# One written-out order of 248 letters in place of slots and places, in a pipelined cross-attention kernel

## What is computed

```python
# layer 0
x = attention(ln(x), ln(x), Wq1, Wkv1, Wo1, bo1) + x      # self-attention, 16 heads of 16, scale 1/8
x = attention(ln(x), ctx,   Wq2, Wkv2, Wo2, bo2) + x      # cross-attention, 16 heads of 16
h = ln(x) @ Wff1 + bff1;  lin, g = split(h)               # 256 -> 2 x 1024
x = (lin * (g * sigmoid(1.702 * g))) @ Wff2 + bff2 + x
# layer 1: one attention of x over the context, with its own projections
q, k, v = x @ Wq + bq, ctx @ Wk + bk, ctx @ Wv + bv       # one head, no scale
out = softmax(q @ k.T) @ v + x
```

## Time and profile before

| | us |
|---|---|
| median of 3 runs (1865.70 to 1873.52) | 1872.56 |
| the profiled execution, own time | 1862.73 |
| its span, first to last instruction | 1860.9 |
| busy in the span: PE | 1640.9 (88%) |
| DVE | 1111.0 (60%) |
| ACT | 978.3 (53%) |
| POOL | 265.7 (14%) |
| mean granted TensorE clock | 0.967 |

### The profile page before, as it was taken

How to read it: one execution, slowest core, us unless ns; L and a number is a source line. 1 busy time by engine, 2 the same in 40 slices (tenths; PEclk the granted TensorE clock), 3 DMA queues, 4 the chain that set the end, 5 groups by cost and what they waited for, 6 DMA issues and landing times.

```text
span 1860.9 us, 33823 instructions
## 1 busy us (share of the span) xinstructions
PE 1640.9 (88%) x12897; PEld 1037.2 (56%) x12897; DVE 1111.0 (60%) x2221; ACT 978.3 (53%) x2024; POOL 265.7 (14%) x344
## 2 busy tenths in 40 slices
PE   6799889898989989898998989899898989897877
PEld 5444444564646556564655656465555656464656
DVE  4556676747576575757656574756657575733332
ACT  3255656554656555565555545565554546554332
POOL 5210411201211020121102012100001010101110
PEclk9999999999999999999999999999999999998988
DMA  6904243335131412436121221335030220302200
GB/s 177 211 27 131 66 76 84 74 79 107 48 70 54 80 47 54 88 72 118 51 66 53 56 61 46 78 78 109 19 76 27 54 63 27 76 21 65 50 29 12
DMA packets 171647, 129.37 MB, mean 70 GB/s; under 512 B 40751, under 2 KB 161885, under 8 KB 171229
## 3 DMA queue, kind: packets, MB, share of 16 engines
q1 hardware_dynamic: 171421, 127.19, 29.2%
q10 hardware_dynamic: 64, 0.02, 0.0%
HBM read 78.92 MB, written 47.71 MB: 68 GB/s over the span
## 4 chain that ended last, share of the span: by engine, by line
PE 65%; DVE 21%; ACT 6%; issue 5%; DMA 2%; SPq 1%; ACTq 0%; POOL 0%; DVEq 0%; POOLq 0%
DVE mxh L1383 10%; PE ps_o L1732 10%; PE ps_last L1649 10%; PE ps_max L1705 9%; PE ps_s L1720 6%; PE ps_last L1658 6%; PE ps_pre L1513 4%; PE ps_cross L1617 3%; PE ps_pre L1521 3%; DVE mx L1307 3%; PE ps_cross L1603 2%; PE ps_last L1521 2%; ACT probs L1096 2%; PE ps_last L1687 2%; DVE hT L1342 1%
## 5 line engine op out<-in xcount | busy, mean ns | idle before, releaser
L1383 DVE TENSOR_REDUCE mxh<-ps_max 128x1 f32<-128x512 f32 x1024 | 667.8, 684 | 379.7 <-PE ps_max L1705 377.6
L1152 ACT ACTIVATE probs<-ps_s 128x512 f32<-128x512 f32 x1024 | 556.0, 598 | 316.3 <-PE ps_s L1720 310.7
L1705 PE MATMUL ps_max<-kst,qst 96*128 96x512 bf16 x1024 | 382.4, 390 | 86.1 <-DVE mxh L1383 71.0
L1720 PE MATMUL ps_s<-qst,kst 98*128 98x256 bf16 x2048 | 319.7, 278 | 1.2 <-ACT probs L1152 0.7
L1732 PE MATMUL ps_o<-probs,vg 128*17 128x256 f32 x4096 | 283.4, 393 | 6.4 <-ACT probs L1152 6.4
L1720 PEld LDWEIGHTS ps_s<-qst,kst 98*128 98x128 bf16 x2048 | 199.1, 99 | 92.2 <-issue 11.6
L1705 PEld LDWEIGHTS ps_max<-kst,qst 96*128 96x128 bf16 x1024 | 97.0, 97 | 229.2 <-DVE mxh L1383 170.2
L1096 ACT ACTIVATE probs<-ps_cross 77x512 f32<-77x512 f32 x224 | 133.5, 596 | 85.1 <-PE ps_cross L1603 85.1
L1732 PEld LDWEIGHTS ps_o<-probs,vg 128*17 128x17 f32 x4096 | 93.8, 98 | 136.6 <-issue 69.2
L1649 PE MATMUL ps_last<-y_hi,wff_hi 128*128 128x256 f32 x448 | 140.6, 314 | 24.5 <-DVE hT L1342 19.3
L1125 ACT ACTIVATE th<-ps_last,b_tanh 128x256 f32<-128x256 f32 x112 | 53.1, 474 | 160.4 <-PE ps_last L1649 160.4
(11 more groups left out here) (265 smaller groups left out, 2014.5 us busy)
## 6 DMA issues: line engine op xcount, KB each, us to landing
parts_s<-qk_parts SPq DMA_DIRECT2D x28, 384.0 KB, 3.1
o_s<-o_sb SPq DMA_DIRECT2D x64, 128.0 KB, 2.1
o_s<-o_sb SPq DMA_DIRECT2D x32, 256.0 KB, 2.2
oT<-o_s SPq DMA_DIRECT2D x62, 128.0 KB
den<-o_s SPq DMA_DIRECT2D x62, 128.0 KB
kst<-parts_s SPq DMA_DIRECT2D x16, 384.0 KB, 5.3
kst<-parts_s SPq DMA_DIRECT2D x48, 128.0 KB, 6.1
qst<-parts_s SPq DMA_DIRECT2D x64, 96.0 KB, 2.7
```

The costliest lines, as they stand in the source:

```text
L1152: nc.scalar.activation(probs[:, step % PR, 2 * pair:2 * pair + 2, :].rearrange("p j q -> p (j q)"), ps_s[pair][:, :], ACT.Exp, scale=SCALE ...
L1383: nc.vector.tensor_reduce(mxh[:, i // 2, i % 2:i % 2 + 1], ps_max[i % 2][:, :], AX_X, ALU.max).then_inc(g_mx, 1)
L1705: mm(ps_max[i % 2][:, :], qst[0:ROWS, h, q * P:(q + 1) * P], kst[0:ROWS, h, k * 512:(k + 1) * 512], start=True, stop=True).then_inc(g_mt, 1)
L1720: last = mm(ps_s[pair][:, j * CH:(j + 1) * CH], kst[:, h, kt * P:(kt + 1) * P], qst[:, h, :], start=True, stop=True)
```

## The change

All the constants of slots and places go. A string, `ORDER`, holds one letter for each thing that any engine does in an iteration: M a max tile, Q the maxima of pairs, T the turn of the maxima (with the negation on DVE and the store of the shift on SP), S one score tile with its exponential, V the value products of two steps, O the copy of a unit's output, p, m, c, l one step of `pre`, `mid`, `cross`, `last`, and for SP o (`store_o`), u (`load_stack` for the next unit of this buffer), x (`load_cross`), d, i, e, f (the loads and the store for the next `last`). Every engine now walks this one string, so DVE and POOL take a step of `last` in the same place as PE does. There are as many letters of each kind as before (64 M, 64 S, 36 c, 26 l, 16 V, 9 m, 8 p, 4 each of Q, T, O, o, u, one each of x, d, i, e, f). Each operation, its waits and its operands stay.

```diff
-PRE_AT, CROSS_AT, LAST_AT = (1, 5, 22), (0, 0, 24), (1, 1, 32)
-CROSS_LOAD, DEN_LOAD, DEN_INV, LAST_LOAD = 26, 25, 27, 29
-SUB = 3
-PV_PLACE, LAST_PLACE = 1, 1
 LEAD = 2
-MAX_LAST, MAX_PAIRED, MAX_TURN = 18, 19, 21
-O_STORE, UNIT_LOAD = 0, 2
+ORDER = (
+    "cMMSSMlSoMSMcSSMlcMSlcVScMM"
+    "SmcllVuMSSMucMSMmSSoMmMScSMlQcVTcp"
+    "SpcSMMlcSOVMcSMSlSMScVcMpS"
+    "SMlVMSpMlcMSucSpMcSMlScMpSMSlcMVM"
+    "ScQlSpSTpcScmcMMlcVMcSMlSMcSMOSclmMu"
+    "SVVMSMSmcMlSoSMmMScMSlMmMMQSlcVTlcMM"
+    "SlcSMSMOVSMcmSMlSclMSMVxcSdM"
+    "SMlSMSMVSMSMSMSiMQeflSVoTVOl"
+)
...
-        def walk(n, flags, setup, pre, mid, cross, last, att_work, max_work, tail, loads=lambda slot: None,
-                 late_last=False):
+        def walk(n, flags, setup, pre, mid, cross, last, work):
...
+            chains = dict(
+                p=pre(n) if has_pre else None, m=mid(n - MID_LAG, has_pre) if has_mid else None,
+                c=cross(n - CROSS_LAG) if has_cross else None, l=last(n - LAST_LAG) if has_last else None)
+            seen = dict.fromkeys(ORDER, 0)
+            for letter in ORDER:
+                k = seen[letter]
+                seen[letter] += 1
+                if letter in work:
+                    work[letter](k)
+                elif letter in chains and chains[letter] is not None:
+                    next(chains[letter])
+                if letter == "S" and k % 2:
+                    for _ in range(setup_steps(n, k // 2)):
+                        next(setup)
...
+                def load_unit(k):
+                    done = first + k - 1
+                    if 0 <= done and done + HG < NU:
+                        load_stack(done + HG)
...
+                def store_unit(k):
+                    if 0 <= first + k - 1 < NU and (flags[2] or att_before):
+                        store_o(first + k - 1)
```

More of the change, by code:

```diff
@@ L113, in stages, with max_tile, max_unit @@
         0 <= n - lag < NCH for lag in (ATT_LAG, MID_LAG, CROSS_LAG, LAST_LAG))
[L116 to L132, removed]
+def max_tile(n, k):
+    unit = HG * (n - ATT_LAG) + k // (2 * PAIRS) + LEAD
+    return (unit if 0 <= unit < NU else None), k % (2 * PAIRS)
+def max_unit(n, k):
+    return max_tile(n, 2 * PAIRS * k)[0]
 def xattn_kernel(nc, t, out):
@@ L445, in run @@
                 body(n, n % 2, stages(n), stages(n - 1)[2], stages(n + 1))
-        def walk(n, flags, setup, pre, mid, cross, last, att_work, max_work, tail, loads=lambda slot: None,
-                 late_last=False):
+        def walk(n, flags, setup, pre, mid, cross, last, work):
             has_pre, has_max, has_att, has_mid, has_cross, has_last = flags
[L453 to L481, removed]
-                    if place == LAST_PLACE and not late_last:
-                        advance(0, slot)
-                    if place == SUB - 1:
-                        advance(2, slot)
-                        if late_last:
-                            advance(0, slot)
-                        for _ in range(setup_steps(n, slot)):
-                            next(setup)
-                        loads(slot)
-                    advance(1, slot, place, SUB)
-            tail()
-            assert all(next(work, None) is None for work, _, _ in chains)
@@ L495, in walk_end @@
+            assert all(next(chain, None) is None for chain in chains.values() if chain is not None)
         def walk_end(mid, cross, last, loads=lambda letter: None):
@@ L950, in body @@
             def body(n, u, flags, att_before, after):
-                walk(n, flags, setup_work, pre, mid, cross, last_by(1 - u), lambda slot, place: None, lambda at: None,
-                     lambda: None, late_last=True)
+                walk(n, flags, setup_work, pre, mid, cross, last_by(1 - u), {})
             head()
@@ L1393, in inverses, with max_pairs @@
-                def inverses(slot):
-                    if after[5] and slot == DEN_INV:
+                    dve.wait_ge(g_mt, unit * 2 * PAIRS + i + 1)
+                    nc.vector.tensor_reduce(mxh[:, i // 2, i % 2:i % 2 + 1], ps_max[i % 2][:, :], AX_X,
+                                            ALU.max).then_inc(g_mx, 1)
+                def max_pairs(k):
+                    unit = max_unit(n, k)
+                    if unit is None:
+                        return
+                    dve.wait_ge(g_mx, (unit + 1) * 2 * PAIRS)
+                    nc.vector.tensor_reduce(mxq[:, :], mxh[:, :, :], AX_X, ALU.max).then_inc(g_mp, 1)
@@ L1722, in scores, with values_of @@
                     last.then_inc(g_s, 1)
-                def values(step):
+                def values_of(step):
                     unit, kt = divmod(step, KT)
```

149 lines of the change are left out of this document (69 added, 80 removed).

## The result

The kernel after takes 1769.99 us (median of 4 runs, 1768.6 to 1780.11), the kernel before, run beside it, 1871.82 (1865.7 to 1873.52): a ratio of 0.9473, with a 95% interval of 0.9432 to 0.9515. The profiled execution took 1771.07 us, with a span of 1769.3.

The account below looks back on a forecast made before the run. PE was taken as the floor, 90 us of a 107.1 us iteration. Gains summed to 55 us, times 0.85 gave 47: 1862.7 to 1816, plus 9.9 for the median, 1825 us; range 1797 to 1863, the forecast's own 1808 to 1840.

Parts of the forecast that it names:

- the start: First max tile to second feed-forward group (l8): DVE stays the bound, more PE work gets done meanwhile; gain 2.2 us an iteration.
- the short gaps with V15: Feed-forward, cross and max tile gaps less DVE blocking, plus the last value products' wait at the iteration's end: 2.9 us.
- the factor of 0.85: Applied to the whole 55 us gain, since a PE late less often gives partners less time: 47 us.
- V15's wait: Iteration's end: value products wait for the last score tiles' exponentials; 1.1 us of PE work between removes it, gain 0.8.
- The gaps of the feed-forward, the cross tiles and the max tiles (1.0, 0.9, 0.7, less 0.5): PE's short waits for hidden tiles, cross exponentials and row maxima shrink by 1.0, 0.9, 0.7 us; DVE blocking at the gate costs 0.5.
- The last step (9.9): Whole kernel: the median was taken to lie 9.9 us above the profiled execution, turning 1816 into 1825.
- Iterations 16 to 20 (3.1) and 5 to 7 (0.8): Without `pre` to fill gaps, 3.1 us each, 15 together; without `last`, only the end gains, 0.8 each, 2 together.
- SP's queue (0.3): SP blocked for much of the iteration, tight only from x to `norm_o` at the end; charged 0.3 us an iteration.
- SP is late: Rival: the end's chain of loads and stores on SP overruns, `norm_o` holds DVE; slower, 1904 us, chance 0.08.
- The tail (0): `walk_end`, behind the last iteration, was said to stay as it is, like the head: no gain or loss.
- more dips: Rival: one more low-clock stretch an iteration where score tiles stand singly, costing 22 us: 1847 us, chance 0.07.
- dips gone: Rival: low-clock stretches vanish because l8 comes with more work done; 22 us more gain, 1803 us, chance 0.05.

Follow-up runs that it names:

- The four corners: Old order with DVE and POOL late for `last` 1861 us, at the common place 1959; new order late 1859, common place 1770.
- e9: Kernel after with the cross chain's end two places earlier, its extra steps beside `last` and `mid` letters, x ahead of i, one turn earlier: 1737.09 us.
- e6: Kernel after, but DVE and POOL take steps of `last` one max tile later: 1859.03 us.
- e1: Kernel after with PE's old order as the one string for all engines: 1958.67 us.
- e15: Kernel after with the steps of `pre` and `mid` at their old slots: 1876.79 us.
- e8: PE's old order as one string for all engines, with each slot's second score tile moved to the middle of its slot: 1954.18 us.
- e2: Kernel after with the second score tile of each slot moved up against the first, as pairs: 1800.05 us.
- e13: Kernel after with the cross chain at its old slots, and SP's o(1), u(1), u(2), u(3) where their waits are done: 1816.05 us.
- e3: Kernel after with x, the four loads of the next cross chain, moved behind c35's store and d: 1763.77 us.

## Why the prediction was wrong

The direction was right, and so were most places. What failed is the size: two terms of the sum, the start (2.2 us, measured 4.3) and the short gaps with V15 (2.9, measured 5.4), and the factor of 0.85 laid on them.

**What held.** PE is the floor, its work 90 us an iteration. V15's wait is gone, and so are the waits for cross exponentials. `norm_o` waits for its sums once in five iterations, for 0.6 us.

**The start (2.2 us).** It gained 4.3: from the first max tile to l8 it takes 26.6 us instead of 28.4, with 22.0 us of PE work in it instead of 19.5. The step that failed is "If DVE stays the bound, l8 comes at about the same time". I had 27.3 us of DVE work by distances between records; DVE is busy 24.8 in that stretch, as the window shows, so 3.6 us were there to be gained. This is the term that I could have read before.

**The gaps of the feed-forward, the cross tiles and the max tiles (1.0, 0.9, 0.7, less 0.5).** From l8 to l14 it takes 29.2 us instead of 34.9, for 27.5 and 31.0 us of work: 2.2 gained. From there to the next iteration it is 42.3 where the end is not disturbed, instead of 44.5, with 1.0 us more work: 3.2 gained. Together 5.4, where I had 2.1 and 0.8 for V15. The sum of the three stretches of before above the floor is 8.9 + 3.9 + 5.1 = 17.9 us, of which my short gaps explained 10. I let the others stand as if nothing could take them away, and part of them went too: a short gap makes not only its own reader late but all that is queued behind it on DVE, ACT and SP. The runs with one chain put back show this: count of gaps 0 to 55 us, measured 97 to 134.

**The factor 0.85.** It goes the wrong way. I argued that a PE that is late less often gives its partners less time; the terms as they stood, 55 us, were already too small for the 92 measured between the profiled executions. The four corners show that the two halves of the change help each other, -2, +98 and -91 us against the old order with late DVE. That a PE which is late less often gives its partners less time is not tested by itself.

**The last step (9.9).** I added to the profiled execution what the median before lay above it. After, the median lies 1.1 us below the profiled execution (1769.99 and 1771.07), so about 10 us of the 55 between 1825 and 1770 say nothing about the order: between the profiled executions the gain is 92 us, between the medians 102.

**Iterations 16 to 20 (3.1) and 5 to 7 (0.8).** Measured 7.2 and 3.6. The first follows from the above. Of the 1.7 us that I took off because `pre` no longer fills the gaps, 0.4 is there (7.6 and 7.2). Iterations 5 to 7 I gave only the end; they have max tiles, score tiles, `mid` and cross steps, and gained at those as well.

**SP's queue (0.3).** The rival "SP is late" named the right chain (x, c35, d, i, e, f) and the wrong member. I took 2.2 us for c35's store, from its median of before; behind x's four loads (384 KB and three of 128) it took 4.8 to 6.3, and the wait came at `den_c`, a step ahead of the one I watched. The sum of that chain was also off by itself: its terms, 1.9, 2.2, 2.1, 0.35, 1.8, 1.9 and 2.7, add up to 13.0 us and not 13.5. The stall costs some 3 us an iteration (slots 30 and 31: 1.0 before, 3.8 after, 0.6 in e9), most of it in every second one: from l14 on these take 46.7 us, the others 42.3. e9 takes it away, moves two cross steps and a turn for it, and gains 33 us; so this order, with its end mended, is worth 135 us.

**The tail (0).** The forecast said that head and `walk_end` stay; they got 2.8 and 12.5 us longer. The windows behind the last score tile, after and before:

```profile
1592.00:1769.00 177.00, 134.81 (x819) 103.14 (x817) 60.85 (x135) 53.28 (x121) 16.67 (x25) 0.81 0.13 35
```

```profile
1697.00:1861.00 164.00, 124.62 (x799) 96.09 (x798) 59.67 (x132) 53.65 (x122) 16.72 (x25) 0.88 0.13 35
```

The granted clock is 0.81 there instead of 0.88, that is, 66 us at the lower level instead of 39, and PE is busy 10 us longer with all but the same work. In the head it is 18 us at the lower level instead of 12. The 18 traces order themselves by this: their tails take 163 to 184 us with 36 to 77 us at the lower level, and grow by 0.47 us for each of these (correlation 0.96). For the 27 us between the two kernels that would be 13. What lowers the clock there is not shown by itself. `walk_end` begins with the steps that need the inverses, where DVE waits 8.5 us for the sums and PE 4.8 for oT, and the first 30 us of the tail are 5 us longer; the rest comes later, in a stretch with 24 us more at the lower level.

**The clock.** Between 322 and 1100 us the granted clock falls to the lower level 8 times before, about once an iteration; 4 times after, right behind the stall at the end of the long iterations; never in e9; 12 times in e6 and 16 times in e1. The dip that I expected in the second half of each start is not there. At the end of the long iterations, and in slot 15 of e15, it falls behind a wait of PE. Breaking up the pairs added none: with pairs and with single tiles it falls 16 and 15 times in the old order (e1, e8), 5 and 4 times in the new one (e2, the kernel after). The rule of the Trainium skill ("TensorE: Matmul & The Clock Gate", the section on psum-queue depth-cycling), as the rival "more dips" read it, would have given more of them. The traces don't agree with this reading. The opposite case, dips gone, had a chance of 0.05; half of them are gone.

What stays open: why o and u at their old slots lengthen iterations 5 to 7 by 10 us, why six max tiles and two turns moved to slots 11 to 23 cost 3.5 us an iteration in slots 8 to 29, where 46 us of e13 over the kernel after lie, and what lowers the clock in the tail.

## What to carry to other kernels

With in-order queues on every engine, the order of all chains is one object: a new order and a new place for one engine can each gain nothing, or cost 5%, and together gain 5%, so try them together, and don't price a reorder by the short gaps alone. When a kernel is 17 us over its floor and your list explains 10, don't take the rest as fixed: here 4.8 were counted and 7.6 went. Check the busy time in the window before you call an engine the bound, and don't put bulk loads ahead of a small store on whose landing a chain waits. An order that mends the steady state can lengthen the ends, so look at head and tail as well.

## What the runs showed of the hardware

In the full iterations of the kernel after, a store of 256 KB issued right behind four loads (768 KB) on the same queue landed in 4.8 to 6.3 us, and in 7.9 and 9.0 where x also loads `k2st` and `v`; with the loads issued later the same store landed in 2.1 us in each iteration of e3, and in 2.2 to 2.4 in all but one of e9 (4.6). The granted clock falls where PE has waited more: 8, 4 and 0 times in some 780 us, with the same matmuls; in the tail, 10 us more of PE's busy time for all but the same matmuls go with 27 us more at the lower level. The same instructions on the same engines take from 1737 to 1959 us by order alone, and PE's busy time for them runs from 1606 to 1682 us.
